# Attention loop: codes made at the head of TensorE's step and copied three tiles ahead

## What is computed

```python
def gnn(h, adjacency, Wq, Wk, Wv):
    q, k, v = h @ Wq.T, h @ Wk.T, h @ Wv.T
    mask = adjacency.T
    scores = jnp.where(mask, q @ k.T, NEG)
    attn = jax.nn.softmax(scores, axis=1)
    attn = jnp.where(mask, attn, 0.0)
    return attn @ v
x = x + gnn(layernorm(x), adj, Wq, Wk, Wv)
x = x + ffn(layernorm(x)[None], W_router, W1, b1, W2, b2)[0]   # 8 experts, top 2
```

## Time and profile before

| | us |
|---|---|
| median of 3 runs | 1002.48 |
| lowest, highest | 999.99, 1002.5 |
| profiled execution, its own time | 1002.19 |
| its span, first to last instruction | 1000.5 |
| mean granted TensorE clock, share of full speed | 0.864 |

### The profile page before, as it was taken

How to read it: one execution, slowest core, us unless ns; L and a number is a source line. 1 busy time by engine, 2 the same in 40 slices (tenths; PEclk the granted TensorE clock), 3 DMA queues, 4 the chain that set the end, 5 groups by cost and what they waited for, 6 DMA issues and landing times.

```text
span 1000.5 us, 23493 instructions
## 1 busy us (share of the span) xinstructions
PE 739.6 (74%) x6471; PEld 664.8 (66%) x6473; DVE 601.1 (60%) x2055; ACT 455.7 (46%) x1281; POOL 443.0 (44%) x498
## 2 busy tenths in 40 slices
PE   1478888888864022644531999999999999999994
PEld 1367777777752022534431998989988988899894
DVE  8545555555544643887330857667676766685654
ACT  3445555555540011032311566565555555566653
POOL 2266666666630431066774233343434333434343
PEclk8569999999997566855555999999999999999997
DMA  9844424441100000153463232314242424212121
GB/s 295 263 121 119 114 54 106 119 116 30 37 18 6 20 0 0 59 167 107 157 224 105 90 119 89 105 54 137 68 139 67 146 66 143 76 51 69 45 69 39
DMA packets 88555, 95.37 MB, mean 95 GB/s; under 512 B 10522, under 2 KB 77602, under 8 KB 88380
## 3 DMA queue, kind: packets, MB, share of 16 engines
q1 hardware_dynamic: 69836, 60.40, 20.5%
q0 software_dynamic: 18672, 34.44, 10.9%
HBM read 82.64 MB, written 28.87 MB: 111 GB/s over the span
## 4 chain that ended last, share of the span: by engine, by line
PE 35%; DVE 21%; issue 17%; POOL 10%; DMA 8%; ACT 8%; DVEq 1%; POOLq 1%; ACTq 0%; SPq 0%
PE psE L1250 9%; POOL expert_in L504 6%; DMA acc<-out,tok_next 4%; DVE prod L644 4%; PE psH L1239 4%; PE psH L1241 4%; PE psH L1240 4%; PE psE L1252 4%; ACT diag L1319 3%; DVE vals L622 2%; POOL out L529 2%; PE psY L1088 2%; PE psX L1226 1%; ACT masks L1326 1%; POOL nbr L469 1%
## 5 line engine op out<-in xcount | busy, mean ns | idle before, releaser
L1428 ACT ACTIVATE z_all<-psH,b1T 128x256 f32<-128x256 f32 x296 | 142.3, 481 | 162.2 <-PE psH L1241 162.2
L459 POOL DMA_INDIRECT nbr<-xn_rows,idx x160 | 160.6, 1004 | 119.1 <-DVE idx L634 75.6
L1250 PE MATMUL psE<-w_parts,h_hi 128*128 128x512 f32 x552 | 209.9, 406 | 3.8 <-DVE h_lo L991 3.2
L1239 PE MATMUL psH<-x_hi,w_hi 128*128 128x256 f32 (+1 forms) x592 | 166.4, 281 | 11.3 <-issue 7.8
L991 DVE TENSOR_TENSOR h_lo<-z_all,h_hi 128x256 fp32r<-128x256 f32 x296 | 122.8, 425 | 82.9 <-ACT h_hi L1429 82.9
L1241 PE MATMUL psH<-x_hi,w_lo 128*128 128x256 f32 (+1 forms) x592 | 166.3, 281 | 0.0
L1240 PE MATMUL psH<-x_lo,w_hi 128*128 128x256 f32 (+1 forms) x592 | 166.1, 281 | 0.0
L1252 PE MATMUL psE<-w_parts,h_lo 128*128 128x256 f32 x552 | 155.1, 281 | 0.0
L1429 ACT ACTIVATE h_hi<-psH,b1T 128x256 fp32r<-128x256 f32 x296 | 141.8, 479 | 0.0
L529 POOL DMA_INDIRECT out<-y_out,tok_now x74 | 78.9, 1067 | 114.0 <-DVE y_out L967 102.6
L1239 PEld LDWEIGHTS psH<-x_hi,w_hi 128*128 128x128 f32 x592 | 112.7, 190 | 22.2 <-issue 14.3
(11 more groups left out here) (290 smaller groups left out, 1281.0 us busy)
## 6 DMA issues: line engine op xcount, KB each, us to landing
adj_in<-in_adj SPq DMA_DIRECT2D x8, 2048.0 KB
w_raw<-in_L_ffn_W SPq DMA_DIRECT2D x16, 1024.0 KB, 5.7
x_in<-expert_in SPq DMA_DIRECT2D x38, 260.0 KB
x_all<-in_x SPq DMA_DIRECT2D x4, 1024.0 KB, 9.0
xn_rows<-z_all SPq DMA_DIRECT2D x4, 1024.0 KB
out<-x_all SPq DMA_DIRECT2D x4, 1024.0 KB, 4.9
nbr<-xn_rows,idx POOLq DMA_INDIRECT x176, 2.4
expert_in<-pad_row SPq DMA_DIRECT2D x8, 260.0 KB, 3.2
```

Source lines behind the costliest of these rows:

```text
L459: pool.indirect_dma_start(nbr[:, u * K + k, :], None, xn_rows, bass.IndirectOffsetOnAxis(ap=idx[:, u, k:k + 1], axis=0), bounds_check=ROW0 ...
L1239: pe.matmul(psH[:, hc % 4, cols], w1_hi[:, b, k, m], x_hi[:, k, cols], start=(k == 0), stop=False)
L1250: pe.matmul(psE[:, q, :], h_hi[:, hc, m], w2_parts[:, b, hc].rearrange("p s c -> p (s c)"), start=(hc == 0), stop=False)
L1428: act.activation(h_f[:, hc, :], psH[:, hc % 4, 0:T], ACT.Relu, bias=b1T[:, e * HC + hc:e * HC + hc + 1])
```

## The change

In TensorE's step, code(t+3) stands right behind degree(t+3), ahead of project(t-2) and weigh(t-1), instead of behind them. ScalarE's step t copies the codes of tile t+3, into the buffer of that tile's parity, instead of those of t+2; ahead of its steps it copies the codes of tiles 0, 1 and 2 instead of 0 and 1. Waits, buffers and the order on the other engines are as they were.

```diff
@@ TensorE, step(t, u, a, uses)
                 if not (over and t + 3 >= NT):
                     wait_alone(pe, deg_copied, t + 1)
                     degree(uses[(u + 3) // GT], (u + 3) % GT, C, (a + (u + 3) // GT) % 2)
+                    code(t + 3, (u + 3) % GT, (a + (u + 3) // GT) % 2)
                 if not (first and t < 2):
                     project(t - 2, t + 1)
                 if not (first and t < 1):
                     weigh(t - 1, (u - 1) % GT)
-                if not (over and t + 3 >= NT):
-                    code(t + 3, (u + 3) % GT, (a + (u + 3) // GT) % 2)
                 if not (over and t + 1 >= NT):
                     query(t + 1)
@@ ScalarE, step(t, u)
-                if not (over and t + 2 >= NT):
-                    read_masks(t + 2, u % 2)
+                if not (over and t + 3 >= NT):
+                    read_masks(t + 3, (u + 1) % 2)
@@ ScalarE, ahead of its steps
-            for t in range(2):
-                read_masks(t, t)
+            for t in range(3):
+                read_masks(t, t % 2)
```

## The result

| | us |
|---|---|
| before, median of 3 runs | 1002.48 (999.99 to 1002.5) |
| changed kernel, median of 3 runs | 976.33 (974.56 to 976.49) |
| ratio, 95% interval | 0.9742 (0.9713 to 0.977) |
| profiled execution of the changed kernel, its own time | 976.49 |
| its span; that of before | 974.8; 1000.5 |

What follows compares the result with a forecast made beforehand. VectorE and ScalarE alternating were taken to bound the attention loop. Start 1.05, steps 4 to 28 27.65 and steps 29 and 30 1.3 sum to 30.0 us off 1002.19: 972.2 us, forecast 969 to 975, whole range 968.5 to 981.

Steps and rivals of the forecast that it cites:

- The bound and the mechanism: Attention loop: VectorE and ScalarE alternate; copying masks a tile earlier removes the search's 2.76 us wait a tile.
- the new wait of ScalarE for codes: ScalarE's codes copy waits for codes TensorE makes in the same step; 0.6 us of cover predicted.
- The step: Attention loop: TensorE's step sums to 6.65 us (6.63 to 6.74), in place of a 7.756 us period.
- the upper bound that step 30 had shown: Transposes behind weigh: 1.01 us to query in step 30 against 0.90, so 0.11 at most added; 0.02 taken.
- Steps 29 and 30: Loop steps without degree and code: 5.8 us each, 11.6 for 12.93 together, 1.3 us won.
- 27.65: Gain in us over steps 4 to 28: 25 steps at 6.65 instead of 7.756.
- one of the prediction's own signs of being wrong: TensorE's granted clock under 1.00 between 75 us and the loop's end would show the prediction wrong.
- the 30.0: Total predicted gain in us: start 1.05, steps 4 to 28 27.65, steps 29 and 30 1.3.
- the mechanism as a rival: Attention loop: TensorE's clock falls, steps of some 10.5 to 11 us, kernel slower; chance 0.03.
- The start: Ahead of step 4: step 1's codes lie inside TensorE's wait for the first diagonals, 1.05 us won.
- Behind the loop: From step 31 on the chain of yT, project and weigh was to stay as it was, no gain.
- GpSimd as the bound: Attention loop: VectorE holds up gathers, 6.85 to 7.05 us a tile, 977 to 982 us; chance 0.17.

Runs made afterwards that it cites:

- fp32 filler: Changed kernel plus one unused fp32 matmul of 256 columns each step where TensorE waits for xT: 984.74 us, ratio 0.9837 to the kernel before.
- f16 filler: Changed kernel plus one unused f16 matmul of 512 columns each step where TensorE waits for xT: 971.84 us, ratio 0.9712 to the kernel before.
- the narrow runs parted: Changed kernel with code(t+3) between project and weigh instead of right behind degree: 973.17 us, ratio 0.9725 to the kernel before; again 973.12 us.
- the order alone: Kernel before with code right behind degree on TensorE, ScalarE still copying two tiles ahead: 1000.32 us, ratio 0.999.
- ScalarE alone: Kernel before with ScalarE copying codes three tiles ahead, TensorE's code still behind weigh: 1052.66 us, ratio 1.0513.
- changed kernel twice: Changed kernel, unaltered, profiled at first measurement (976.33 us) and again beside other kernels: 976.25 us, ratio 0.9749 to the kernel before.
- four gathers: Changed kernel with four gathers a tile instead of five, so its output differs: 973.9 us, ratio 0.9723 to the kernel before.
- fillers in every second and fourth step: Changed kernel with the unused f16 matmul of 512 columns only in every second step (980.62 us) or every fourth (973.25 us).

## Why the prediction was right, and where not

**The bound and the mechanism** were as read. The search's wait went, the chain moved to TensorE, the new wait of ScalarE for codes held nothing up (codes end 194.3, the copy begins 195.00 in the step from 192.33: 0.7 us of cover, 0.6 predicted). The two halves need each other: alone, one made it 5% slower, the other nothing.

**The step** came out at 6.65, as predicted to the hundredth, and that was luck in its parts. The code loads take 0.80 us behind degree (241.52 to 242.32), not 0.90; the transposes, with weigh in front of them, take 1.01 to the query (245.41 to 246.42), not the 0.92 that I took, but the upper bound that step 30 had shown. The two errors of 0.1 cancel. The bound from step 30 was not the product of its waiting for diagonals, as I argued.

**Steps 29 and 30** took 5.83 each (248.03 to 253.86, for one), predicted 5.8.

**The step that failed is that all 25 would be so.** Three fell to half clock: 4.95 us, the term missing from 27.65. So the steady period held in 22 of 25 steps, and one of the prediction's own signs of being wrong, a granted clock under 1.00 in the loop, did come. By the span 4.3 us of the 30.0 are missing: 4.95 of the falls and 1.3 behind the loop, less 1.96 that the start gave beyond its sum.

I had the mechanism as a rival, in the form that 27% of the steps or more run slowly, at some 4 us each, where 12% did at 1.65, and dismissed it with "the new order leaves TensorE less idle". That argument looks at idle time alone.

The runs show that in the steady loop neither a wait of 0.52 us nor the narrow matmuls alone is enough: with the wait filled (fp32 filler) or shortened to 0.30 (f16 filler) the traces have no fall but those behind a stopped back edge, and with the narrow runs parted none either, at the same wait; put together as in the change there are two or three, as in the order alone five. Neighbours are not the only way to a fall: with more idle time (ScalarE alone, 1.14 and 0.46 us) the clock is low for much of the loop, though degree and code do not follow each other there.

Which of the stretches of the same content falls is not told by any row, but the falls are not scattered: where two follow each other with nothing but steps of 6.65 us between them, they are nine or ten steps (61.5 or 68.1 us) apart in every trace (changed kernel twice, four gathers, fillers in every second and fourth step). What sets that distance stays open. The Trainium skill (TensorE: Matmul & The Clock Gate, "Part 1") has the gate follow how busy the array was lately. The profile's busy share does not tell these falls: it is 1.00 in the microsecond ahead of the one shown above.

**The start** gave 3.01 instead of 1.05. Weight loads of the changed kernel:

```profile
57.18 3.83 PEld L1088 LDWEIGHTS psY<-diag,nbr 128*128 128x128 f32 x20 [4.87 <-ACT diag L1318]
...
62.69 1.06 PEld L1060 LDWEIGHTS psT<-unit,adj_in 128*128 128x128 fp8e4 x32
...
75.99 1.06 PEld L1060 LDWEIGHTS psT<-unit,adj_in 128*128 128x128 fp8e4 x32
```

Step 2 begins at 62.69, in before at 64.08: the codes inside the wait, and a little. The rest is that before then ran at a granted clock of 0.57 from 65 to 69 us and the changed kernel at 1.00: step 2 took 8.29 us there and 6.65 here, where the prediction took step 2 of before for one like step 3 (6.63). It is a fall of the same price as the three, on the other side of the account, but with degree and code apart, and behind TensorE's long wait. In the second trace of the changed kernel step 4 begins at 76.75, a gain of 2.25.

**Behind the loop** 1.3 us were lost between the loop's end and the span's, in stages the change doesn't touch; the table above shows that such differences come with other edits too. Over the first 30 us there the granted clock was 0.70 before and is 0.68 now; the cause stays open.

**GpSimd as the bound** (0.17) did not come about, though its gathers fill its time. The Trainium skill's rule (SBUF — State Buffer, "Who interferes with whom"), that VectorE's two-port instructions and GpSimd exclude each other for a whole instruction, is seen in kind and not in size. VectorE's instructions and GpSimd's gathers as groups, 75 to 240 us of the changed kernel (count, busy us, mean ns, idle before):

```profile
L459 POOL DMA_INDIRECT nbr<-xn_rows,idx x124 | 127.4, 1027 | 37.8 <-issue 36.3 <-DVE idx L634 1.5
...
L636 DVE COPY masks_all<-masks 128x512 bf16 (+1 forms) x25 | 8.3, 332 | 0.0
L635 DVE COPY vals_all<-vals 128x5 f32 (+1 forms) x25 | 6.5, 260 | 0.0
...
L628 DVE TENSOR_SCALAR name_u<-vals 128x5 uint32<-128x5 uint32 x24 | 3.8, 158 | 0.0
```

name_u, 351 ns before, is back at 158, and the two copies behind it are longer (vals_all 260 for 170, masks_all 332 for 294): the place of the meeting moved, and the delay is 0.1 us on average and not an instruction's length. The timelines show which part of a gather it is. In before 23 of the 24 name_u begin 0.57 to 0.70 us into a gather, and all 23 end 0.97 us into it. In the changed kernel the 14 vals_all that begin 0.55 to 0.78 us into a gather end 0.97 us into it too, and the seven that begin elsewhere in one (0.32 to 0.54, 0.87 and 0.90) take 0.17 us, as before. So a VectorE instruction is held up in a part of the gather alone, by 0.25 us at most. The gathers took 1027 ns for 999, 0.14 us a tile, which keeps GpSimd at 6.65 and level.

## What to carry to other kernels

When a ring of waits between two engines is opened, sum the next engine's step from its loads in order and expect that step, but look at what the engine's clock will do in the new order: short narrow matmuls put side by side next to idle time cost three falls of 1.65 us here, and parting the two runs by a wide product took them away for 0.09 us a step. A copy that is sent ahead on an in-order queue needs its producer moved ahead as well: one half alone cost 5%. Before a filler or any other instruction is added to an unrolled loop body, look at the back edges of the trace for waits behind "issue" and at the packets of the instruction queue.

## What the runs showed of the hardware that was not expected

- The granted clock falls to 0.50 while the profile has TensorE busy all the time, behind 64 matmuls of 1 and 16 columns that follow a wait of 0.52 us: 3 to 4 us, 1.65 us lost each. All six falls of the partly filled kernels come behind an unfilled wait.
- 4 to 32 instructions more in TensorE's loop body: with 4, no stop; with 8, 16 and 32, in one trace of each, one or two back edges where TensorE stands for 5 to 5.7 us in two pieces (3.0 to 3.5 and 1.9 to 2.2), 9 instruction packets each, and the clock falls behind it.
- A run of 32 narrow loads takes 0.80 us behind another narrow run and 0.99 behind fp32 matmuls of 256 columns.
- A gather of 1.00 us on GpSimd holds up a small VectorE instruction (128x5, 0.15 to 0.17 us by itself) that begins 0.6 to 0.78 us into it until 0.97 us into it; one that begins 0.1 to 0.5 us into it runs unhindered.
- Kernels that differ only in the attention loop differ by up to 4 us in the 705 us behind it (702.5 to 706.5).
